# Gathered segment sums on TensorE: the fixed and the moving operand exchanged

## What is computed

```python
msg_in   = concatenate([nodes[senders], edges], -1)      # 256 + 64 features an edge
agg      = segment_sum(msg_in @ W_message, receivers)    # first graph layer
h        = layer_norm(relu(agg) + nodes)
nodes    = layer_norm(nodes + mlp(h))                    # 3 layers of 256x256
# then a mixture of 16 experts, a sparse projection, and a second graph layer,
# which takes the mean over the incoming edges of the gathered rows,
# and a mixture of 8 experts
```

## Time and profile before

| | |
|---|---|
| median of 3 runs | 1449.61 us (1449.51 to 1450.31) |
| profiled execution: span from first to last instruction | 1607.9 us (its own device time is not given apart from this) |
| PE busy, mean granted clock of the span | 1175.4 us (73%), 0.825 |
| DVE, ACT, POOL busy | 709.5, 661.1, 746.3 us |
| stage O0: first and last gather begin | 43.0 and 476.6 us |
| stage O1: first and last products of a group | 1045.2 and 1341.4 us |

### The profile page before, as it was taken

The page is one execution under the profiler, slowest core; times in us unless marked ns, Lnnn a source line. Parts: engine busy times, 40 slices in busy tenths (PEclk is TensorE's granted clock), DMA queues, the critical chain, the costliest instruction groups (busy, mean ns, idle before and its releaser), DMA issues. The chain is left out here.

```text
span 1607.9 us, 27179 instructions
## 1 busy us (share of the span) xinstructions
PE 1175.4 (73%) x7129; PEld 1007.4 (63%) x7130; DVE 709.5 (44%) x2376; ACT 661.1 (41%) x1842; POOL 746.3 (46%) x841
## 2 busy tenths in 40 slices
PE   1287788887899739999993777377778867478780
PEld 1277777876789628999992333166557666367670
DVE  7133455655446761111114999334433225522225
ACT  3554555654113333444443555576651002323230
POOL 5655555655550004222215776366456660266650
PEclk9977888877989958999996999755678885588885
DMA  5543344444440047999992232433223332422227
GB/s 173 147 112 107 107 109 115 118 114 105 112 115 25 17 160 254 350 352 352 349 322 85 85 89 72 132 90 95 76 76 103 97 94 70 133 78 78 81 75 249
DMA packets 186771, 220.03 MB, mean 137 GB/s; under 512 B 69103, under 2 KB 148503, under 8 KB 186382
## 3 DMA queue, kind: packets, MB, share of 16 engines
q1 hardware_dynamic: 148240, 125.81, 24.4%
q0 software_dynamic: 32352, 87.30, 18.7%
q10 hardware_dynamic: 6046, 5.40, 1.1%
HBM read 187.33 MB, written 32.19 MB: 137 GB/s over the span
## 5 line engine op out<-in xcount | busy, mean ns | idle before, releaser
L783 POOL DMA_INDIRECT O0G<-n_rows,src_tab x260 | 251.1, 966 | 194.5 <-PE O0ps_sums L802 91.8
L783 POOL DMA_INDIRECT O1G<-sparse_rows,src_tab x188 | 180.0, 958 | 125.9 <-issue 58.7
L802 PE MATMUL O0ps_sums<-O0OH,O0G 128*128 128x80 f32 x1040 | 160.1, 319 | 1.3 <-issue 1.2
L802 PEld LDWEIGHTS O0ps_sums<-O0OH,O0G 128*128 128x128 f32 x1040 | 153.7, 234 | 6.3 <-issue 2.7
L802 PEld LDWEIGHTS O1ps_sums<-O1OH,O1G 128*128 128x128 f32 x752 | 122.9, 251 | 14.1 <-issue 10.2
L1982 POOL DMA_INDIRECT e0xs<-token_rows,e0idx x60 | 56.8, 947 | 159.7 <-ACT e0idx L2071 155.9
L802 PE MATMUL O1ps_sums<-O1OH,O1G 128*128 128x80 f32 x752 | 123.3, 333 | 9.8 <-issue 7.4
L2027 PE MATMUL e0ps_h<-e0xT,e0W 128*128 128x128 f32 x1024 | 126.7, 277 | 0.8 <-ACT e0xT L2077 0.8
L2122 DVE TENSOR_TENSOR e0ys<-e0ps_y,NR 128x256 f32<-128x256 f32 x64 | 27.2, 425 | 215.3 <-PE e0ps_y L2041 215.3
L2027 PEld LDWEIGHTS e0ps_h<-e0xT,e0W 128*128 128x128 f32 x1024 | 121.1, 194 | 1.5 <-issue 1.4
L2041 PE MATMUL e0ps_y<-e0W,e0hidT 128*128 128x256 f32 x512 | 120.9, 379 | 0.0
(11 more groups left out here) (382 smaller groups left out, 2701.5 us busy)
## 6 DMA issues: line engine op xcount, KB each, us to landing
e0W<-in_L_ffn_w SPq DMA_DIRECT2D x128, 512.0 KB
O0EA<-in_edge_attr SPq DMA_DIRECT2D x97, 128.0 KB
expert_out<-e0ys SPq DMA_DIRECT2D x64, 128.0 KB
O0G<-n_rows,src_tab POOLq DMA_INDIRECT x260
e1W_all<-in_L_ffn_w SPq DMA_DIRECT2D x16, 256.0 KB, 6.0
n_rows<-NR SPq DMA_DIRECT2D x5, 640.0 KB
token_rows<-O0N SPq DMA_DIRECT2D x25, 128.0 KB
m0own<-token_rows SPq DMA_DIRECT2D x25, 128.0 KB
```

The costliest lines, as they stand in the source:

```text
L783: pool.indirect_dma_start(out=self.G[:, s, k, :], out_offset=None, in_=self.rows_dram, in_offset=bass.IndirectOffsetOnAxis(ap=src_tab[:, g ...
L802: last = nc.tensor.matmul(self.ps[o % 2][0:rows.shape[1], half * P:half * P + WINDOW], rows, self.OH[:, h, k, 0:WINDOW], start=(k == 0), s ...
```

## The change

The products of a gathered group are exchanged: the one-hot of a tile (80 columns) is the fixed operand and the gathered row (256 columns) the moving one, so that the four tiles of a group are summed in one place of a bank as 80 nodes by 256 features; in O0 four more matmuls move the 65 columns of the edge features beside it. ACT then copies the 80x321 (O1: 80x256) sums out of PSUM into `R`, PE turns them in three (two) transposes into a third bank, `ps_turned`, and DVE adds from there with one add, as before.

```diff
@@ products
-                if o >= 2:
-                    pe.wait_ge(self.added, o - 1)
-                if n is not None:
-                    for half in range(self.halves):
-                        for k in range(GC):
-                            rows = self.EA[:, e, k, :] if half == 2 else self.G[:, r, k, half * P:(half + 1) * P]
-                            last = nc.tensor.matmul(self.ps[o % 2][0:rows.shape[1], half * P:half * P + WINDOW], rows, self.OH[:, h, k, 0:WINDOW],
-                                                    start=(k == 0), stop=(k == GC - 1))
+                if o >= 2:
+                    if self.is_gathered(o - 2):
+                        pe.wait_ge(self.copied, self.gathered_before(o - 1))
+                    else:
+                        pe.wait_ge(self.added, self.adds_before(o - 1))
...
+                    for k in range(GC):
+                        last = nc.tensor.matmul(bank[0:WINDOW, 0:D], self.OH[:, h, k, :], self.G[:, n % self.GR, k, :],
+                                                start=(k == 0), stop=(k == GC - 1))
+                    for k in range(GC) if self.with_edges else ():
+                        last = nc.tensor.matmul(bank[0:WINDOW, D:D + DE + 1], self.OH[:, h, k, :], self.EA[:, e, k, :],
+                                                start=(k == 0), stop=(k == GC - 1))
...
+            def copy(self, act, o):
+                if self.is_gathered(o):
+                    n = self.gathered_before(o)
+                    act.wait_ge(self.summed, o + 1)
+                    if n >= 2:
+                        act.wait_ge(self.turned, n - 1)
+                    nc.scalar.activation(self.R[0:WINDOW, n % 2, :], self.ps[o % 2][0:WINDOW, 0:self.row_cols], ACT.Copy).then_inc(self.copied, 1)
+
+            def turn(self, pe, o):
+                if o >= 0 and self.is_gathered(o):
+                    n = self.gathered_before(o)
+                    pe.wait_ge(self.copied, n + 1)
+                    if n >= 1:
+                        pe.wait_ge(self.added, self.adds_before(self.plan.gathered[n - 1] + 1))
+                    for part in range(self.halves):
+                        cols = min(P, self.row_cols - part * P)
+                        last = nc.tensor.transpose(self.ps_turned[0:cols, part * P:part * P + WINDOW], self.R[0:WINDOW, n % 2, part * P:part * P + cols],
+                                                   ident[0:WINDOW, 0:WINDOW])
+                    last.then_inc(self.turned, 1)
...
@@ add, of a gathered group
-                dve.wait_ge(self.summed, o + 1)
+                dve.wait_ge(self.turned, self.gathered_before(o) + 1)
...
@@ PE's part of a slot, and ACT's
                         for o in parts(groups_of(u), q):
+                            sums.turn(pe, o - 1)
                             sums.products(pe, o)
...
                                     adjacency.hot(act, v + HOTS - 1)
+                                for o in parts(groups_of(u), q):
+                                    sums.copy(act, o)
...
@@ NodeMlp: the bank of the gate logits is given up
-                self.ps_agg, self.ps_tn, self.ps_01, self.ps_2, self.ps_bg = (
-                    pb(f"{tag}ps_{n}", [P, 512], c) for n in ("agg", "turned", "0_1", "2", "back"))
+                self.ps_agg, self.ps_tn, self.ps_01, self.ps_2 = (
+                    pb(f"{tag}ps_{n}", [P, 512], c) for n in ("agg", "turned", "0_1", "2"))
+                self.ps_bg = self.ps_2[:, D:D + E0]
...
                     wait_tile(pe, S["z_ready"], t, 1)
+                    wait_tile(pe, S["logits_in"], t, 3)
...
                     wait_tile(pe, S["nT_ready"], t)
-                    wait_tile(pe, S["logits_in"], t, 1)
+                    wait_tile(pe, S["z_ready"], t, -2)
...
@@ NeighbourMeans
-                self.ps_s, self.ps_n, self.ps_g = (pb(tag + n, [P, 512], c) for n in ("ps_s", "ps_n", "ps_g"))
+                self.ps_s, self.ps_n = (pb(tag + n, [P, 512], c) for n in ("ps_s", "ps_n"))
+                self.ps_g = self.ps_n[:, D:D + E1]
...
-                    wait_tile(pe, S["nT_ready"], t, 1)
+                    wait_tile(pe, S["logits_in"], t, 1)
...
@@ load_edges: a tile is 128 edges in a row, no longer every fourth edge
-                sp.dma_start(to, rows.rearrange("(p c) f -> p c f", c=GC)).then_inc(self.edges_in[s], 16)
+                sp.dma_start(self.EA[:, s, 0:full, 0:DE], a["edge_attr_64"][g * GE:g * GE + full * P, :].rearrange("(c p) f -> p c f", p=P)).then_inc(self.edges_in[s], 16)
...
@@ route, on POOL and ACT: the matrix `before` is made here, no longer at the start of the program
+                    nc.gpsimd.memset(before[:], 1.0)
...
+                    nc.gpsimd.affine_select(out=before[:], in_=before[:], compare_op=ALU.is_gt, fill=0.0,
+                                            base=0, pattern=[[1, P]], channel_multiplier=-1).then_inc(s_earlier, 1)
...
+                    act.wait_ge(s_earlier, 1)
                     nc.scalar.activation(before_b[:], before[:], ACT.Copy).then_inc(s_ones, 1)
```

More of the change, by code:

```diff
@@ L50, in build @@
     E_LAST = E_N - (NG - 1) * GE
-    P_LAST = E_LAST // GC
-    assert P_LAST * GC == E_LAST
+    C_LAST, REST = divmod(E_LAST, P)
+    assert 0 < REST and C_LAST < GC and REST % 16 == 0
     WIN = NPAD + P
@@ L247, in build @@
         ones = sb("ones", [P, P])
-        before = sb("before", [P, P])
         iota_w = sb("iota_w", [P, P])
@@ L278, in build, with once_nodes_done @@
         w_nodes = sb("w_nodes", [P, K2, D])
+        after_nodes, taken_after = w_nodes[:].rearrange("p k n -> p (k n)"), [0]
+        def once_nodes_done(rows, *sizes, dt=F32):
+            first = taken_after[0]
+            taken_after[0] += int(np.prod(sizes))
+            assert taken_after[0] <= K2 * D
+            cols = after_nodes[0:rows, first:taken_after[0]]
+            cols = cols if dt == F32 else cols.bitcast(dt)
+            names = "abc"[:len(sizes)]
+            return cols.rearrange(f"p ({' '.join(names)}) -> p {' '.join(names)}", **dict(zip(names, sizes))) if len(sizes) > 1 else cols
+        logit1 = once_nodes_done(P, T, E1)
+        top_w = once_nodes_done(P, T, 2)
+        slot = once_nodes_done(P, T, 2, dt=I32)
+        token = once_nodes_done(P, max(NB0, NB1), dt=I32)
+        dest = once_nodes_done(P, NB1, dt=I32)
+        block_expert = once_nodes_done(1, max(NB0, NB1), dt=I32)
         w_edges = sb("w_edges", [DE + 1, D + 1])
@@ L476, in _ @@
                 for c in range(3):
-                    last = nc.tensor.matmul(ps_e[0:1, c * P:c * P + NG], ends[:, c:c + 1], ident[0:NG, 0:NG], start=True, stop=True)
+                    last = nc.tensor.matmul(ps_e[0:1, c * NG:(c + 1) * NG], ends[:, c:c + 1], ident[0:NG, 0:NG], start=True, stop=True)
                 last.then_inc(s_rowp, 1)
@@ L660, in wait_tile @@
             n = ((t.n if isinstance(t, Turn) else t) + 1 - ago) * per
+            if isinstance(n, int):
+                n = min(n, T * per)
             if not (isinstance(n, int) and n <= 0):
@@ L788, in products @@
                 h, e = o % HR, o % ER
-                n = self.plan.gathered.index(o) if o in self.plan.gathered else None
-                r = n % self.GR if n is not None else None
                 pe.wait_ge(self.hot_ready, o + 1)
@@ new lines, in products @@
+                bank = self.ps[o % 2]
+                if self.is_gathered(o):
+                    n = self.gathered_before(o)
+                    pe.wait_ge(self.gathered[n % self.GR], (n // self.GR + 1) * 16 * GC)
+                    for k in range(GC):
[4 more added lines that the diff above has]
+                                                start=(k == 0), stop=(k == GC - 1))
@@ L916, in piece, with join @@
                     last.then_inc(self.passed, 1)
-            def join(self, dve, q, sums_added, groups):
+            def join(self, dve, q, sums):
                 half_pass = PIECES // 2
@@ L923, in join @@
                 dve.wait_ge(self.passed, q // half_pass + 1)
-                dve.wait_ge(sums_added, groups)
+                dve.wait_ge(sums.added, sums.adds_issued)
                 window = sumT[:, 0:K2, base:base + n]
@@ L1266, in group @@
                         for o in parts(groups_of(u), q):
+                            sums.turn(pe, o - 1)
                             sums.products(pe, o)
-                    return group
-                def groups_added(u, q):
-                    if u >= plan.sum_steps:
-                        return sums.groups
-                    return max(plan.groups_by[u] + min(q + 1, len(groups_of(u))) - 1, 0)
+                        if u == plan.sum_steps and q == 0:
+                            sums.turn(pe, sums.groups - 1)
+                    return group
                 def joined_by(u, q):
@@ L1289, in group @@
                             for i in parts(pieces_of(u), q):
-                                adjacency.join(dve, i, sums.added, groups_added(u, q))
```

(3 more changed lines are left out.)

110 lines of the change are left out of this document (62 added, 48 removed).

## The result

The changed kernel takes 1503.31 us (median of 4 runs, 1501.3 to 1505.41), the kernel before 1449.96 us on the same chip. The ratio is 1.0365, with a 95% interval of 1.0344 to 1.0387: slower by 53 us, outside the range of the forecast. Slower had the largest chance in the forecast, but the time lies beyond even the slow rival's price (1492 us).

What follows compares the result with a forecast made beforehand. PE was taken as nearest its limit, much of it at 1.2 GHz, with POOL's gathers behind. Terms summed to +10 us of profile time, +9 us of 1449.61: 1459 us; range 1424 to 1492 us, likeliest case 1453 to 1474.

Steps and rivals of the forecast that it cites:

- slow rival: O0 and O1: sums going PE, ACT, PE, DVE put copy and turn on the path; 1492 us, chance 0.20.
- PE's columns: O0 and O1: PE's products, turns and other work, with the low clock's share falling by a third; -13 us.
- The turn behind the group: O0's last slots with two groups: turn waits for ACT's copy, delaying DVE's adds; 0.7 us each, +8 us.
- The late groups: Late O1 and late O0, no piece between group and turn: 0.4 us on some ten, +4 us (0 to 12).
- ACT's copy: O1 steps with counts: next one-hots stand behind the copy in ACT's queue; 0.55 us over 11 steps, +6 us.
- The gate's bank: O0: gate logits share the third layer's bank, so PE's logits wait for z; +4 us (0 to 17).
- The matrix: Routing stages: `before` is made on POOL ahead of ACT's copy, PE's first product may wait; +1 us (0 to 4).
- B: O0 and O1: the four-engine chain has copy and turn on the path for 60% of groups; 1492 us, chance 0.20.
- A: O0 and O1: the dense stream keeps PE's clock up, low share halves or more; 1434 to 1410 us, chance 0.33.
- The mark set for A: Sign against the forecast: PE's granted clock in O0 going above 0.92.
- The mark for B: Sign against the forecast: PE's idle time in front of counts and turns growing by over 30 us.

Runs made afterwards that it cites:

- the surroundings: Changed kernel with products, add and waits as before, no copy or turn; shared gate bank, edge-load order and other changes stay: 1461.84 us.

## Why the prediction was wrong

Its sum was -13 + 6 + 8 + 4 + 4 + 1 = +10 us of profile time. By the runs it is about -27 for the exchange without its turns, +68 for copy and turn in both stages, and +9 for the surroundings.

*PE's columns*, -13: this term holds the turns' time on PE, which the run of -27 leaves out. Without the turns (0.43 us a group in O0 and 0.30 in O1 at the forecast's shares) the same sum is -20 - 14 - 25 = -59, of which 80% are -47, or -42 us of device time. So the sign was right, and the gain of the exchange was put too high by half. A group at 2.4 GHz was put at 1.72 + 0.55 + 0.33 us; the timeline of PE after shows 1.76 us for the products, 0.56 for the edge rows and, by the starts, 0.21 for three turns:

```profile
250.81 1.93 PE L830 MATMUL O0ps_sums<-O0G,O0OH 128*80 128x256 f32 x8
252.57 0.72 PE L833 MATMUL O0ps_sums<-O0EA,O0OH 128*80 128x65 f32 x8
253.13 1.11 PE L1553 MATMUL O0ps<-O0hT,w_mlp 128*128 128x128 f32 x8
...
256.35 0.38 PE L859 MATMUL O0ps_sums_turned<-ident,O0OH 80*128 80x80 f32 x3
256.56 1.89 PE L830 MATMUL O0ps_sums<-O0G,O0OH 128*80 128x256 f32 x8
```

So the price of the turns on PE was too high, if anything. The 275 ns that the forecast set against its 110 ns are another thing: one of these turns lasts 242 ns by the mean of its rows (ends are modelled), but they overlap, and PE pays the distance of their starts.

*The turn behind the group*, +8: **this is the step that failed.** The forecast saw the right queue, DVE's add into `adj` behind the add that waits for the turn. It priced this for the last slots with two groups and put the other slots at nothing, since a piece of the node network "covers copy and hops" there. The piece covers them for PE, but PE's turn stands behind that piece, and DVE and its add into `adj` wait for the turn. While counts run O0 loses 37.8 us by the table (its rows without copy and turn and of the changed kernel add up to 273.9 and 311.7): 17.5 behind slot 1's count, 10.5 in slot 0, slot 2 and the other last slots, and 9.8 in the eight last slots with two groups, 1.2 us each instead of 0.7. An exchange in the first three slots alone takes slot 1 from 54.8 to 32.6 us, and one in all slots gives 34 us, of which some 17 are the turn's. Part of the 37.8 us is PE's own time for turns, by an estimate from rows 65 x 0.21 = 14 us in all of O0, and 8.6 us are PE's waits for the copy; no run takes these apart from DVE's wait. A kernel with PE's turn ahead of the piece was not run.

*The late groups*, +4: from the last count to the last product O0 takes 86.8 us instead of 80.7 without copy and turn, and O1 106.3 instead of 104.7. These 8 us lie within the bounds.

*ACT's copy* in O1, +6: the mechanism was right, the size was not. The term took 0.55 us for eleven steps, as if one slot of a step lost. Every slot with a group has the wait, 24 of the 47 groups while counts run, and the copies alone cost 16 us, whole or of one column. The bound of 1.45 x 11 = 16 us that stood beside it was met, but by chance, as it too counted one slot a step. With the turns the part of O1 with counts is 20 us longer (132.9 to 152.6).

*The gate's bank*, +4: 8 us, within its bounds. *The matrix* and the rest, +1: 1462 - 1459 = 3 us, within what the runs can tell.

The rivals. B, the chain of four engines, was the right one, at +42 us; the true price of copy and turn is 68 us, since it counted their latency on the path and not what stands behind them on DVE and ACT. A was right that the exchanged products keep the clock higher (0.84 against 0.67 in O1 while counts run, without copy and turn), and wrong in that this decides. The mark set for A, a clock above 0.92 in O0, came true (0.93 and 1.00, 0.94 in all) without A: the kernel before has 0.90 and 1.00 there, 0.92 in all, in its second profile. The mark for B, over 30 us more idle time of PE before counts and turns, came true: 60.6 to 72.2 us before counts in O0, 8.7 before turns; in O1 44.9 to 62.8 before counts and 5.2 before turns.

A premise failed as well: that the first profile's stages are typical and can be scaled by 0.90. By the mean record in O0 the forecast put the low clock's share at 43%. In the second profile it is

```profile
L802 PE MATMUL O0ps_sums<-O0OH,O0G 128*128 128x80 f32 x1040 | 139.9, 293 | 0.1
```

139.9 / 1040 = 135 ns, by the same rule 24%. The page and the timed times did not agree by 158 us, and that was the warning.

## What to carry to other kernels

When work is moved to an engine that works in order, price what stands behind the new wait in that engine's queue, in every slot, and not the work: a copy of one column cost as much as a whole one. Ask also where the operation that ends the wait stands in its own engine's order: here a turn came 2 us after its copy was out. A repair that moves an unrelated operation ahead of the wait gave more here than the faster products did, and should be tried with the old products first: it was 17 us there, in the surroundings of the change (1444.72 us, 7 us under the kernel before; on that kernel itself it was not run). And if the span of a profile and the timed runs differ, take another profile ahead of any sum.

## What the runs showed of the hardware

One profiled execution of the kernel before spanned 1607.9 us and another 1444.9 us, with mean clocks of 0.825 and 0.869; why, no run shows. At 2.4 GHz eight float32 records with 80 fixed and 256 moving columns took 1.76 us (220 ns each), and sixteen with 128 fixed and 80 moving ones 1.77 us (111 ns): half the records and the same time. Eight with 65 fixed and 80 moving columns take 0.55 us (69 ns), and eight with 80 fixed and 65 moving ones 0.56 us (70 ns). In these four shapes the time goes with the larger of the two sides, some 0.87 ns a column. In O1 with counts the clock was 0.67 with the old products and 0.84 with the exchanged ones without copy and turn, for the same counts, as these two rows show (the surroundings alone, then without copy and turn):

```profile
972.40:1114.70 142.30, 116.60 (x578) 97.36 (x578) 67.68 (x178) 109.43 (x240) 92.24 (x98) 0.67 0.34 98
```

```profile
958.60:1091.50 132.90, 98.41 (x385) 62.99 (x385) 67.47 (x178) 108.79 (x240) 92.02 (x98) 0.84 0.36 105
```
